# adaLN block (SSM mixer and RWKV-style channel mix): first modulation columns and the composed front weights put in another order at the kernel's start

## What is computed

```python
mod = (silu(c) @ wmod).reshape(16, 6, 1, 256)          # sa, ca, ga, sb, cb, gb; the two gates are kept at least 0.25 in size
h = layernorm(x) * (1 + ca) + sa
u, gate = split(h @ W_in.T)
b = u @ W_state.T
dt = minimum(softplus(u @ W_dt.T + b_dt), 10)
decay = exp(-dt * (softplus(A_log) + 1e-4))
state_t = decay_t * state_(t-1) + (1 - decay_t) * b_t   # over the 512 tokens
x = x + ga * (((state @ W_C.T) * silu(gate) + h * D) @ W_out.T)
h = layernorm(x) * (1 + cb) + sb
xr, xk = mixtures of h and h shifted by one token (mu_r, mu_k)
x = x + gb * (sigmoid(xr @ W_r.T) * (relu(xk @ W_k.T)**2 @ W_v.T))
```

## Time and profile before

| | |
|---|---|
| median of 3 runs | 343.72 us (343.62 to 874.88) |
| the profiled execution | 343.59 us, span 341.8 us |
| granted TensorE clock, mean | 0.998 |
| PE busy | 335.0 us (98%) |
| DVE, ACT, POOL busy | 303.6, 292.4, 275.5 us |
| DMA | 36.00 MB, mean 105 GB/s |

### The profile page before, as it was taken

The page is one execution under the profiler, slowest core; times in us unless marked ns, Lnnn a source line. Parts: engine busy times, 40 slices in busy tenths (PEclk is TensorE's granted clock), DMA queues, the critical chain, the costliest instruction groups (busy, mean ns, idle before and its releaser), DMA issues.

```text
span 341.8 us, 5185 instructions
## 1 busy us (share of the span) xinstructions
PE 335.0 (98%) x1574; PEld 265.4 (78%) x1574; DVE 303.6 (89%) x465; ACT 292.4 (86%) x393; POOL 275.5 (81%) x274
## 2 busy tenths in 40 slices
PE   8999998999999999999999999999999999999995
PEld 4567676788888888888888888888888888887764
DVE  3789888999999999999999999999999989887846
ACT  4486778989999999999999998999999999888484
POOL 2151879989898998989899898989899896966752
PEclk9999999999999999999999999999999999999999
DMA  7960523060513406051421505151320501010013
GB/s 276 416 226 13 172 83 104 1 221 27 186 61 112 136 18 221 11 186 63 161 85 64 186 0 186 63 186 61 102 83 14 174 3 61 1 63 0 2 60 126
DMA packets 18556, 36.00 MB, mean 105 GB/s; under 512 B 4960, under 2 KB 5728, under 8 KB 18400
## 3 DMA queue, kind: packets, MB, share of 16 engines
q1 hardware_dynamic: 17808, 35.19, 29.7%
q10 hardware_dynamic: 720, 0.48, 0.5%
HBM read 27.22 MB, written 8.44 MB: 104 GB/s over the span
## 4 chain that ended last, share of the span: by engine, by line
PE 89%; DVE 5%; issue 3%; ACT 2%; POOL 0%; DVEq 0%; ACTq 0%; POOLq 0%
PE slot L293 71%; PE slot L386 4%; PE slot L300 4%; PE slot L537 2%; PE slot L528 2%; PE slot L527 2%; PE slot L307 1%; PE slot L314 1%; PE slot L333 1%; DVE xk L979 1%; DVE xr L979 1%; DVE xn L945 1%; PE slot L394 1%; DVE h L940 0%; ACT prev L663 0%
## 5 line engine op out<-in xcount | busy, mean ns | idle before, releaser
L1173 POOL TENSOR_TENSOR k_lo<-k_act,k_hi 128x512 fp32r<-128x512 f32 x30 | 50.2, 1694 | 4.5 <-ACT k_act L872 4.5
L663 ACT ACTIVATE prev<-slot,mod,mix_prev 128x512 f32<-128x512 f32 x64 | 46.4, 785 | 1.3 <-PE slot L300 0.7
L293 PE MATMUL slot<-h_hi,wf_hi 128*128 128x512 f32 x120 | 43.0, 399 | 0.1
L1173 POOL TENSOR_TENSOR xr_lo<-xr,xr_hi 128x512 fp32r<-128x512 f32 x32 | 42.7, 1337 | 0.2 <-ACT xr_hi L709 0.2
L293 PE MATMUL slot<-h_hi,wf_lo 128*128 128x512 f32 x120 | 41.9, 390 | 0.0
L1173 POOL TENSOR_TENSOR xk_lo<-xk,xk_hi 128x512 fp32r<-128x512 f32 x30 | 38.6, 1315 | 3.7 <-ACT xk_hi L703 3.7
L1232 POOL TENSOR_TENSOR h_lo<-h,h_hi 128x512 fp32r<-128x512 f32 x28 | 36.5, 1305 | 1.3 <-ACT h_hi L684 1.3
L1294 POOL TENSOR_TENSOR z_lo<-z,z_hi 128x512 fp32r<-128x512 f32 x26 | 33.3, 1303 | 2.7 <-ACT z_hi L858 2.7
L293 PE MATMUL slot<-h_lo,wf_hi 128*128 128x512 f32 x120 | 34.2, 389 | 0.0
L979 DVE SCALAR_TENSOR_TENSOR xk<-slot,mix_new,prev 128x512 f32<-128x512 f32 x32 | 23.8, 746 | 8.2 <-issue 7.9
L945 DVE TENSOR_SCALAR xn<-slot,stats,rstd 128x256 f32<-128x256 f32 x62 | 29.2, 532 | 0.0
(11 more groups left out here) (164 smaller groups left out, 977.6 us busy)
## 6 DMA issues: line engine op xcount, KB each, us to landing
x_ch<-x_ch_in SPq DMA_DIRECT2D x16, 512.0 KB, 4.3
x_tok<-x_tok_in SPq DMA_DIRECT2D x15, 512.0 KB, 5.4
x_out<-wmod SPq DMA_DIRECT2D x15, 512.0 KB, 3.2
spread_rows<-rows_spread SPq DMA_DIRECT2D x13, 512.0 KB, 3.8
wmod<-wmod_in SPq DMA_DIRECT2D x1, 1024.0 KB, 8.5
w_in<-weights_in SPq DMA_DIRECT2D x1, 1024.0 KB, 11.2
w_in<-weights_in SPq DMA_DIRECT2D x1, 512.0 KB, 4.5
wmod<-wmod_in SPq DMA_DIRECT2D x1, 512.0 KB, 5.8
```

The source lines that it names most:

```text
L293: ins = nc.tensor.matmul(out, w[:, c, at + d * P:at + (d + 1) * P], x[:, c, :], start=first, stop=last)
L663: return nc.scalar.activation(prev[:, mix, i, 1:T + 1], ps_n[:, i, :], ACT.Identity, bias=mod_at(SHIFT2 + i, k), scale=mix_prev[:, mix, i, ...
L1173: nc.gpsimd.tensor_tensor(lo, x, hi.bitcast(F32), ALU.subtract).then_inc(done, 1)
```

## The change

SP issues the first `wmod` columns ahead of `w_early`'s first part. PE makes the modulation columns first, then only the `dt` half of the composed weights (`composed(0)`, 4 matmuls with 128 columns, slot 1), then the transposes, then the `b` half (`composed(1)`, slot 3) where the two zero matmuls stood; `b` of sequence 0 waits for a second `front_ok`. DVE copies the halves out one by one, with the two first `rate` operations between them, and takes over from POOL the addition of eps; POOL takes minus the mean from DVE, behind the power. ACT's exp and ln of `rate` come behind both halves of `h`.

```diff
--- before.py
+++ after.py
@@ -154,6 +154,9 @@
         def ps_x1(k):
             return (slot[2] if k == 0 else slot[1] if k < LAST else slot[0])[:].rearrange("p a b -> p (a b)").rearrange("p (t c) -> p t c", t=TT)
 
+        def ps_composed(q):
+            return slot[1] if q == 0 else slot[3]
+
         def ps_v(k):
             return slot[1] if k < LAST else slot[2]
 
@@ -241,10 +244,10 @@
                 sp.dma_start(spread_rows[:, k % 2], rows1_d[k].partition_broadcast(P)).then_inc(s_row_in[k % 2], 16)
 
             sp.dma_start(x_tok[:, 0, 0:TT // 2], x_tok_d[0, :, 0:TT // 2]).then_inc(s_xt[0], 16)
+            wmod_cols = wmod_d.rearrange("(c p) n -> p c n", p=P)
+            sp.dma_start(wmod[:, :, 0:2 * C], wmod_cols[:, :, 0:2 * C]).then_inc(s_wmod, 16)
             w_early_d = w_d[:, 0:CH * 3 * C].rearrange("p (c n) -> p c n", c=CH)
             sp.dma_start(w_early[:, :, 0:GATE], w_early_d[:, :, 0:GATE]).then_inc(s_w, 16)
-            wmod_cols = wmod_d.rearrange("(c p) n -> p c n", p=P)
-            sp.dma_start(wmod[:, :, 0:2 * C], wmod_cols[:, :, 0:2 * C]).then_inc(s_wmod, 16)
             sp.dma_start(w_early[:, :, GATE:], w_early_d[:, :, GATE:]).then_inc(s_wgate, 16)
             load_tokens(1)
             sp.dma_start(w_y, w_d[:, CH * 7 * C:]).then_inc(s_wy, 16)
@@ -388,15 +391,18 @@
 
             pe.wait_ge(zeros_ok, 1)
             keep_warm(slot[0][:, 0, :], 10)
-            pe.wait_ge(s_w, 16)
-            for m in range(CH):
-                for c in range(CH):
-                    last = nc.tensor.matmul(slot[1][:, m, 0:2 * NS], w_early[:, c, IN_U + m * P:IN_U + (m + 1) * P], w_early[:, c, DT_STATE:DT_STATE + 2 * NS],
-                                            start=(c == 0), stop=(c == CH - 1))
-            last.then_inc(front_ps, 1)
+            def composed(q):
+                for m in range(CH):
+                    for c in range(CH):
+                        last = nc.tensor.matmul(ps_composed(q)[:, m, 0:NS], w_early[:, c, IN_U + m * P:IN_U + (m + 1) * P],
+                                                w_early[:, c, DT_STATE + q * NS:DT_STATE + (q + 1) * NS], start=(c == 0), stop=(c == CH - 1))
+                last.then_inc(front_ps, 1)
+
             pe.wait_ge(s_wmod, 16)
             pe.wait_ge(csilu_ok, 1)
             modulation(0, 4, slot[2][:, 0, :]).then_inc(mod1_ps, 1)
+            pe.wait_ge(s_w, 16)
+            composed(0)
             pe.wait_ge(s_id, 16)
             pe.wait_ge(xn1a_ok, 1)
             pe.wait_ge(xn1b_ok, 1)
@@ -404,13 +410,14 @@
                 for t in range(TT):
                     last = nc.tensor.transpose(ps_h(0)[:, c, t * P:(t + 1) * P], xn1[:, t, c * P:(c + 1) * P], ident[:])
                 last.then_inc(t1_half_ps if c == 0 else t1_ps, 1)
-            keep_warm(slot[3][:, 0, :], 2)
+            composed(1)
 
             pe.wait_ge(front_ok, 1)
             pe.wait_ge(h0_ok, 1)
             half(dt_out, w_front, 0, h[:, 0], 0, first=True)
             pe.wait_ge(h_ok, 1)
             half(dt_out, w_front, 0, h[:, 0], 1, last=True).then_inc(dt_ps, 1)
+            pe.wait_ge(front_ok, 2)
             half(b_out, w_front, NS, h[:, 0], 0, first=True)
             half(b_out, w_front, NS, h[:, 0], 1, last=True).then_inc(b_ps, 1)
             pe.wait_ge(s_wgate, 16)
@@ -641,10 +648,6 @@
             act.wait_ge(s_c, 16)
             nc.scalar.activation(c_silu[:], c_sb[:], ACT.Silu).then_inc(csilu_ok, 1)
             nc.scalar.preload_act_table_set("natural_log_exp_and_others")
-            act.wait_ge(rate_step, 2)
-            nc.scalar.activation(rate[:, 1:2], rate[:, 0:1], ACT.Exp, scale=-1.0).then_inc(rate_exp, 1)
-            act.wait_ge(rate_exp, 1)
-            nc.scalar.activation(rate[:, 2:3], rate[:, 1:2], ACT.Ln, bias=1.0).then_inc(rate_ln, 1)
 
             def gate(k):
                 act.wait_ge(r_ps, k + 1)
@@ -730,6 +733,10 @@
             modulated(0, 0).then_inc(h0_ok, 1)
             act.wait_ge(t1_ps, 1)
             modulated(0, 1).then_inc(h_ok, 1)
+            act.wait_ge(rate_step, 2)
+            nc.scalar.activation(rate[:, 1:2], rate[:, 0:1], ACT.Exp, scale=-1.0).then_inc(rate_exp, 1)
+            act.wait_ge(rate_exp, 1)
+            nc.scalar.activation(rate[:, 2:3], rate[:, 1:2], ACT.Ln, bias=1.0).then_inc(rate_ln, 1)
             exponential(0)
             decays(0)
             nc.scalar.preload_act_table_set("silu_and_others")
@@ -1045,18 +1052,20 @@
             ln1_stats(0)
             ln1_mean_variance(0)
             dve.wait_ge(mv1_ok, 1)
-            nc.vector.tensor_scalar(spread1[:, 0, 0, :], mv1[:, 0, :, 0], -1.0, None, ALU.mult).then_inc(minus1_ok, 1)
-            dve.wait_ge(s_cols, 16)
-            nc.vector.tensor_scalar(rate[:, 1:2], col(A_LOG), -1.0, None, ALU.mult).then_inc(rate_step, 1)
-            dve.wait_ge(rate_step, 1)
-            nc.vector.tensor_tensor(rate[:, 0:1], rate[:, 1:2], col(A_LOG), ALU.max).then_inc(rate_step, 1)
+            nc.vector.tensor_scalar(spread1[:, 0, 1, :], mv1[:, 0, :, 1], EPS, None, ALU.add).then_inc(spread1_ok, 1)
             ln1_first()
             dve.wait_ge(mod1_ps, 1)
             chained(mod_step, nc.vector.tensor_copy(mod[:, 0:4, :], slot[2][:, 0, 0:4 * NB].rearrange("p (j b) -> p j b", b=NB)))
             nc.vector.tensor_scalar(mod[:, 2:4, :], mod[:, 2:4, :], 1.0, None, ALU.add).then_inc(mod1_ok, 1)
             dve.wait_ge(front_ps, 1)
-            nc.vector.tensor_copy(w_front[:], slot[1][:, :, 0:2 * NS]).then_inc(front_ok, 1)
-            dve.wait_ge(front_ok, 1)
+            nc.vector.tensor_copy(w_front[:, :, 0:NS], ps_composed(0)[:, :, 0:NS]).then_inc(front_ok, 1)
+            dve.wait_ge(s_cols, 16)
+            nc.vector.tensor_scalar(rate[:, 1:2], col(A_LOG), -1.0, None, ALU.mult).then_inc(rate_step, 1)
+            dve.wait_ge(rate_step, 1)
+            nc.vector.tensor_tensor(rate[:, 0:1], rate[:, 1:2], col(A_LOG), ALU.max).then_inc(rate_step, 1)
+            dve.wait_ge(front_ps, 2)
+            nc.vector.tensor_copy(w_front[:, :, NS:], ps_composed(1)[:, :, 0:NS]).then_inc(front_ok, 1)
+            dve.wait_ge(front_ok, 2)
             nc.vector.tensor_copy(wf_hi[:, :, 0:2 * NS], w_front[:])
             dve.wait_ge(s_wgate, 16)
             nc.vector.tensor_copy(wf_hi[:, :, 2 * NS:], w_early[:, :, GATE:GATE + C]).then_inc(wsplit_hi, 1)
@@ -1179,12 +1188,13 @@
                 before(pool, xn1b_ok, k - 1)
                 if k > 0:
                     nc.gpsimd.tensor_scalar(spread1[:, k % 2, 0, :], mv1[:, k % 2, :, 0], -1.0, None, ALU.mult)
-                nc.gpsimd.tensor_scalar(spread1[:, k % 2, 1, :], mv1[:, k % 2, :, 1], EPS, None, ALU.add).then_inc(spread1_ok, 1)
+                    nc.gpsimd.tensor_scalar(spread1[:, k % 2, 1, :], mv1[:, k % 2, :, 1], EPS, None, ALU.add).then_inc(spread1_ok, 1)
                 pool.wait_ge(spread1_ok, k + 1)
                 nc.gpsimd.tensor_tensor(rstd1[:, k % 2], spread1[:, k % 2, 1, :], half_neg[:], ALU.pow).then_inc(rstd1_ok, 1)
+                if k == 0:
+                    nc.gpsimd.tensor_scalar(spread1[:, 0, 0, :], mv1[:, 0, :, 0], -1.0, None, ALU.mult).then_inc(minus1_ok, 1)
+                    pool.wait_ge(minus1_ok, 1)
                 pool.wait_ge(rstd1_ok, k + 1)
-                if k == 0:
-                    pool.wait_ge(minus1_ok, 1)
                 nc.gpsimd.tensor_tensor(shift1[:, k % 2], spread1[:, k % 2, 0, :], rstd1[:, k % 2], ALU.mult).then_inc(shift1_ok, 1)
 
             def ln1_rows(k):
```

## The result

The changed kernel takes 345.27 us (median of 20 runs, 343.45 to 347.43), the kernel before 343.93 (20 runs beside them; 343.84 without the run of 874.88): ratio 1.0044, 95% interval 1.0027 to 1.0062. It is slower, by 1.3 us where 0.2 less was forecast, and the median lies outside the range of 342.8 to 344.5.

What follows compares the result with a forecast made beforehand. PE, busy 98%, bounds the kernel, its start hanging on composition, modulation, transposes and half an `h`. Of 0.6 won, DVE's lag leaves 0.2: 343.59 - 0.2 = 343.4 profiled, 343.5 against the median; range 342.8 to 344.5.

Steps and rivals of the forecast that it cites:

- Loads, tokens, PE up to the product: Kernel start: swapped loads and earlier modulation bring PE's first product to about 10.4 instead of 10.98, 0.6 us won.
- the end of the range at 0.24 an instruction: Composed halves on PE: 1.05 more per half, state 1.6 later, 345.2; chance 0.05 shared with the swap-fails rival.
- What is late next: DVE's queue behind the second copy: clip 0.43 later, PE waits 0.34 before the state output, 0.26 of 0.6 remains.
- Rival A: DVE's lag at the start does not matter, the whole 0.6 gain stays: 343.0; chance 0.18.
- Carrying it to the end: 0.2 us carried through the start; from 36 us on the shift passes to the end, with nothing enlarging it.
- The clock: PE's start: light modulation directly behind the zeros and two fewer zero matmuls were taken to cost no granted clock.
- Rival C: Clock falls back before PE's first products, which run at half rate: 2.2 us lost, 345.6; chance 0.05.
- Rival B: `w_early`, loaded in third place, lands late and delays transposes through state; at 0.9 late 343.95; chance 0.17.
- D: Load swap does not land `wmod` earlier (7.43), state 1.2 later, 344.8; chance 0.05 shared with a slow half composition.

Runs made afterwards that it cites:

- e15: The changed kernel run once more, unaltered: 345.38 us, ratio 1.0036 to the kernel before.
- e14: Changed kernel with twelve starting zero matmuls instead of ten and DVE's clip ahead of sequence 1's statistics, repeated in another job: 343.17 us, ratio 0.9969.
- e9: Changed kernel with twelve zero matmuls at the start instead of ten, nothing else: 344.11 us, ratio 1.0014 to the kernel before.
- e7: Changed kernel with twelve starting zero matmuls instead of ten and DVE's clip ahead of sequence 1's statistics, first job: 343.49 us, ratio 0.9970.
- e4: Changed kernel with DVE's clip of sequence 0 ahead of the statistics of sequence 1: 345.11 us from six runs, ratio 1.0038.
- e1: Kernel before with modulation columns loaded and made first, composition whole behind them, both zero matmuls kept: 344.10 us, ratio 1.0027.
- e6: Changed kernel with six more zero matmuls, one behind each of four modulation columns and two behind the dt half: 344.56 us, ratio 1.0044.
- e8: Changed kernel with two zero matmuls behind modulation, two behind the dt half, and DVE's clip ahead of sequence 1's statistics: 343.99 us, ratio 1.0008.
- e3: Changed kernel with four more zero matmuls, two behind the modulation and two behind the dt half: 344.40 us, ratio 1.0039.

## Why the prediction was wrong

**Loads, tokens, PE up to the product.** Right at the full clock, in part by luck. Forecast and e15's profile: dt half 7.45 and 7.68, transposes 8.59 and 8.66, first product 10.4 and 10.42. The modulation started 0.13 late and took 1.85 instead of 1.70, but the tokens were there at 8.34, so the wait of 0.28 that I had put ahead of the transposes was missing; the two nearly cancel. The untried half composition takes 0.89 from transposes' end to product (10.42 - 9.53), against 0.86 from the nearest row; the end of the range at 0.24 an instruction was not needed at the full clock.

**What is late next.** Right: second copy 10.55 and 10.62, clip 14.78 and 14.85, PE's wait 0.34 and 0.28, state output 19.00 and 19.07; silu of the gate 19.27 and 19.26. The 0.6 us won on PE shrinks to 0.19 at the state output (19.26 to 19.07), and there it is DVE's queue that takes it. e14's profile shows that, with the clip first, no wait, and state output at 18.87; so do the runs: with the clip first the kept runs fall from a median of 343.98 (e9) to 343.35 (e7, another job), while the same edit does nothing to the kernel before. Rival A's 343.0 is where e4's one kept run (343.0) and e7's best (342.9) lie.

**Carrying it to the end.** The 0.2 cannot be seen: the kept run's span is 341.9 against 341.8, and the 8 kept runs have a median of 343.85 beside a kernel before whose own runs spread from 343.4 to 344.5. In e15's profile the product that stands at 36.76 before starts at 36.69: of the 0.19 only 0.07 is left by then, so the step by which the shift passes to the end unchanged was too hopeful. Both are smaller than that spread.

**The clock.** This step failed, and it alone put the median outside the range: all 8 kept runs lie inside it. The term for the granted clock was put at nothing, because the trace of before has a longer light stretch without a loss. That stretch came at 21.85, after 11 us made up mostly of 512-column products. The one the change makes comes directly behind the zeros. In this kernel what PE did before changed what a light stretch cost (e1, e6, e9), and the order was exactly what the change altered. What the runs showed in place of nothing: first product at 11.94 in the fallen profile and 14.01 in the late one (e4's), against 10.42 in the kept one, so 1.5 and 3.6 us; 24 of 32 runs are of these two kinds.

Rival C named the clock, gave it 0.05, and stood at 345.6, above the end of my range at 344.5. That price lies among the fallen runs (345.0 to 345.9) by luck. C put the half rate on the products from 10.98 on, and its sign was more than 0.43 for each of them. In the profile after, the low level lies ahead of them, from 8.0 to a little before 11.5, and the eight products go at 0.43 each, so the sign I had named would have said no. C also gave the two missing zeros as a reason, and e1, which has them, falls all the same. The late runs, at 347, were in no rival.

The rule of the Trainium skill that I weighed ("TensorE: Matmul & The Clock Gate", part 4, transposes not counting as busy in the way matmuls do) is not what acted in the profile after: the fall comes at 8.0, a microsecond before the first transpose at 9.03. Nor was PE idle there: it had no gap from 6.0 on. Whether transposes also keep the clock down is not tested here. The Trainium skill says on the same page, in part 1, that the point at which the clock rises differs from run to run; our zeros agree, ten of them filling 3.92 us in the profile after and 4.45 in the earlier trace rows. I should have drawn from it that one trace of before cannot bound this risk.

**Rival B** (a late load) did not occur in the changed kernel's profiles: `w_early` landed at 7.22 in the profile after. It can occur: in e7's profile it landed at 8.2. **D** did not occur in any profile.

## What to carry to other kernels

When a start is reordered, check what stands directly behind the warming matmuls: a microsecond or two of matmuls with very few columns there can cost far more, in some executions, than the order gains, even if PE is never idle. Look at the distribution of the runs and not at one profile or the median, and don't trust a mean granted clock near 1 for the first microseconds: compare the time of an instruction with that of the same instruction later. When a critical engine is moved earlier, look for the in-order queue that its next input stands in, since a copy that arrives later in front of it hands the gain back.

## What the hardware showed that I had not expected

- The clock fell to 1.2 GHz while PE was busy without a gap (6.0 to 8.0 us in the profile after), the work being 16-column matmuls with their weight loads and then the first 128-column ones.
- The granted clock is recorded as 1.00 through an opening that runs at half pace (e4, to 12.5 us), and nearly all of the longest runs have the highest mean, 0.999.
- Two bf16 zero matmuls more at the start, 0.43 us at the full clock, took the late group from 9 of 32 to none of 36, and the fallen from 15 to 4 (e7, e9, e14).
- The same ten zeros fill 3.70 to 4.45 us in different executions, and behind them an early rise went with a fall under the light modulation (after, e8), a rise at their end with none (e1, e3, e15).
